# Short GpSimd steps behind each scatter of a routed result and behind some scatters in attention

## The reference

```
x = x + layernorm(attention(layernorm(x)))        # 16 heads, 4 key/value groups, rotary, causal softmax
h = layernorm(x)
gate = sigmoid(h @ gate_w + gate_b)               # 16 experts
values, chosen = top_k(gate, 2)                   # two experts per token, values scaled to sum 1
routed = sum over the two of value * (silu(h @ eg) * (h @ eu)) @ ed
x = x + layernorm(h + shared_mlp(h) + routed)
```

## Time and profile before

| | |
|---|---|
| median of 3 runs | 2366.59 us (2365.68 to 2369.12) |
| span of the profiled execution | 2472.9 us |
| the profiled execution's own time outside its span | not given by the page |
| busy share PE, DVE, POOL, ACT | 93%, 78%, 69%, 57% |
| mean granted TensorE clock | 0.980 |
| indirect DMAs issued by POOL | 256 in attention, 286 in the experts |

### The profile page before, as it was taken

One profiled execution on the slowest core, in us unless ns is written; L12 is line 12 of the kernel. 1 busy time (PEld: TensorE's weight loads), 2 busy tenths in 40 slices (PEclk: granted clock), 3 DMA queues, 4 the chain that ended last, 5 costly groups with the idle time before them and its releaser, 6 DMA issues.

```text
span 2472.9 us, 57907 instructions
## 1 busy us (share of the span) xinstructions
PE 2296.5 (93%) x17882; PEld 1478.5 (60%) x17882; DVE 1931.5 (78%) x5142; ACT 1399.3 (57%) x3208; POOL 1697.4 (69%) x2893
## 2 busy tenths in 40 slices
PE   5999999999999999999999999998789899999997
PEld 2565555555555555555555555554668787777754
DVE  6788888888888888888898888975455454677778
ACT  1565666656666566665666665665344454444444
POOL 4556777677776777777777767753656676777776
PEclk7999999999999999999999999998999999999999
DMA  4544445554455544445443444332344466788877
GB/s 133 136 140 147 144 133 156 155 165 138 138 155 146 165 137 142 133 138 157 122 132 111 141 137 129 113 100 70 114 142 146 136 190 201 250 278 283 273 257 253
DMA packets 289486, 391.76 MB, mean 158 GB/s; under 512 B 28000, under 2 KB 237920, under 8 KB 289056
## 3 DMA queue, kind: packets, MB, share of 16 engines
q1 hardware_dynamic: 263168, 316.72, 43.3%
q0 software_dynamic: 26016, 71.34, 7.9%
HBM read 186.84 MB, written 182.75 MB: 149 GB/s over the span
## 4 chain that ended last, share of the span: by engine, by line
PE 51%; POOL 26%; issue 8%; DVE 8%; ACT 3%; DMA 1%; another core or an unknown queue 1%; SPq 1%; POOLq 0%; ACTq 0%; DVEq 0%
PE bank L1710 9%; PE ps_a L859 6%; PE bank L1724 5%; PE ps_out L873 5%; PE ps_d L843 5%; PE ps_d L896 4%; POOL q_parts L683 4%; PE ps_d L889 4%; POOL sorted_dram L770 3%; PE bank L1691 3%; DVE roped_q L1124 3%; POOL rest L685 2%; POOL q_parts L685 2%; POOL guess L739 2%; PE ps_a L861 2%
## 5 line engine op out<-in xcount | busy, mean ns | idle before, releaser
L986 ACT ACTIVATE probs<-ps_a 128x512 f32<-128x512 f32 (+1 forms) x1408 | 713.1, 558 | 434.4 <-PE ps_a L861 339.4
L1109 DVE TENSOR_REDUCE negmax<-ps_d 128x2 f32<-128x768 f32 (+3 forms) x768 | 773.0, 1031 | 138.8 <-PE ps_d L845 73.8
L859 PE MATMUL ps_a<-qs,ks 99*128 99x512 bf16 (+3 forms) x2048 | 515.9, 302 | 19.2 <-ACT probs L986 15.6
L843 PE MATMUL ps_d<-ks,qs 96*128 96x128 bf16 (+3 forms) x2048 | 488.0, 304 | 22.1 <-DMA qs<-q_stack_dram 10.8
L845 PE MATMUL ps_d<-mask_max,ident_bf 128*128 128x128 bf16 x2048 | 394.9, 222 | 0.0
L861 PE MATMUL ps_a<-mask_exp,ident_bf 128*128 128x128 bf16 x2048 | 388.1, 220 | 0.0
L1621 POOL DMA_INDIRECT y_dram<-ysb,to_row x286 | 286.3, 1001 | 98.4 <-issue 53.5
L873 PE MATMUL ps_out<-probs,va 128*32 128x512 f32 (+3 forms) x4096 | 331.9, 442 | 4.1 <-DVE by_token L1159 4.1
L859 PEld LDWEIGHTS ps_a<-qs,ks 99*128 99x128 bf16 x2048 | 199.4, 98 | 202.7 <-ACT probs L986 66.6
L843 PEld LDWEIGHTS ps_d<-ks,qs 96*128 96x128 bf16 x2048 | 202.7, 99 | 191.1 <-DVE negmax L1109 40.6
L770 POOL DMA_INDIRECT sorted_dram<-h,slot x256 | 268.6, 1049 | 66.3 <-issue 65.4
(11 more groups left out here) (209 smaller groups left out, 4253.1 us busy)
## 6 DMA issues: line engine op xcount, KB each, us to landing
qs<-q_stack_dram SPq DMA_DIRECT2D x128, 384.0 KB
rows<-sorted_dram SPq DMA_DIRECT2D x286, 129.0 KB
y_in<-y_dram SPq DMA_DIRECT2D x32, 1024.0 KB
q_stack_dram<-q_parts SPq DMA_DIRECT2D x64, 384.0 KB, 3.0
x_in<-in_x SPq DMA_DIRECT2D x32, 512.0 KB, 4.3
q_stack_dram<-q_parts SPq DMA_DIRECT2D x64, 256.0 KB, 3.2
h_dram<-h SPq DMA_DIRECT2D x32, 512.0 KB
h<-h SPq DMA_DIRECT2D x32, 512.0 KB
```

Source lines behind the costliest of these rows:

```text
L843: pe.matmul(ps_d[:, number % 2, at:at + width], qs[0:KR, b % 2, h, j * P:(j + 1) * P], ks[0:KR, b % 2, g, 0:width], start=True, stop=False)
L859: pe.matmul(ps_a[:, number % 3, at:at + width], ks[0:KM, b % 2, g, j * P:(j + 1) * P], qs[0:KM, b % 2, g * HG + h0 + k, j * P:T], start=Tr ...
L986: act.activation(probs[:, at:at + nh * width], ps_a[:, number % 3, 0:nh * width], ACT.Exp) \
L1109: dve.tensor_reduce(negmax[:, g // 2, j, at:at + nh], src, AX_X, ALU.max, negate=True) \
```

## The change

A class `Spacing` issues a number of 1x1 steps on GpSimd. Each waits for the one before it (its own semaphore `spaced`), none waits for another engine or for a DMA. Two such steps follow the scatter of block j = 1 of every batch, and in the last two batches the scatters of all four blocks. One step follows each of the 286 scatters of a routed result. Nothing else is moved, and no other engine's program changes.

```
+class Spacing:
+    def __init__(self, pool, cell, zeros, done):
+        self.pool, self.cell, self.zeros, self.done, self.n = pool, cell, zeros, done, 0
+
+    def __call__(self, steps):
+        for _ in range(steps):
+            if self.n:
+                self.pool.wait_ge(self.done, self.n)
+            self.pool.tensor_tensor(self.cell, self.zeros, self.zeros, ALU.add).then_inc(self.done, 1)
+            self.n += 1
...
-        pool_cell, dve_cell = sb("pool_cell", [1, 2]), sb("dve_cell", [1, 2])
+        pool_cell, dve_cell = sb("pool_cell", [1, 3]), sb("dve_cell", [1, 2])
...
-        doubled = sem("doubled")
+        doubled, spaced = sem("doubled"), sem("spaced")
...
-        prepare_experts, tile_turn, rest_of_experts = gpsimd_experts(pool)
+        space = Spacing(pool, pool_cell[:, 2:3], zero_col[0:1, 0:1], v["spaced"])
+        prepare_experts, tile_turn, rest_of_experts = gpsimd_experts(pool, space)
...
                     out=sorted_dram[b // SPLIT_AT][:, :], in_=h2[:, k, j, :], in_offset=None,
                     out_offset=bass.IndirectOffsetOnAxis(ap=slot[b % 2][:, j, k:k + 1], axis=0),
                 ).then_inc(scattered[b % 2], 16)
+            if j == 1 or b >= B - 2:
+                space(2)
...
                 out=y_dram[:, :], in_=ysb[:, k, :], in_offset=None,
                 out_offset=bass.IndirectOffsetOnAxis(ap=to_row[k][:, 0:1].bitcast(U32), axis=0),
             ).then_inc(y_stored[k], 16)
+            space(1)
```

More of the change, by code:

```diff
@@ L1606, in sync_experts, with gpsimd_experts @@
         return turn, rest
-    def gpsimd_experts(pool):
+    def gpsimd_experts(pool, space):
         pause = Pause(pool, v["pool_cell"][:, 1:2], zero_col[0:1, 0:1], paused)
```

## The result

The changed kernel runs in 2370.28 us (median of 17 runs, 2367.15 to 2372.61), the kernel before, on the same chip, in 2365.68 us (17 runs, 2363.46 to 2369.12). The ratio is 1.0020, 95% interval 1.0014 to 1.0027: slower by 4.6 us, just about the 0.2% that a measurement can tell. My forecast was faster by 35 us. The time lies outside the forecast's own range (2308 to 2362) and inside the wider one (2303 to 2372) only because that one took in the first rival; it moved the other way than I forecast. And the profile says nearly the opposite of the runs.

The account below looks back on a forecast made before the run. Late signals behind POOL's close indirect DMAs were taken to delay line 687, which ends each attention batch. Gain 59 less 0.4 made 58.6 us of span; 0.6 of it, 35 us, off 2366.6 gave 2332 us, range 2308 to 2362.

Parts of the forecast that it names:

- first rival: Whole kernel: nothing to gain in the runs, only +0.4 us of cost, so 2367 us; chance 0.33.
- From the profiled execution to the runs: Step from profile to timed runs: of a possible 0 to 58.6 us, took 0.6, 35 us, giving 2332 us.
- late signals: PE's completions reaching VectorE and ScalarE late behind POOL's close indirect DMAs; waits of 77 + 20 = 97 us.
- What bounds the kernel: Attention, 52.0 us per batch: line 687's start ends last, released by POOL's root behind late moments and the second rotary product.
- The gain: Gaps let PE's signals through: 29 x 1.7 = 49 us in attention, 10 us at its end, 59 at most.
- The rule against the gain: DMA never contends with a compute engine at SBUF's ports; by it the gain is nil, 2367.0 us.
- The price of a pair: Two steps between two scatters in attention cost POOL about 0.44 us, between 0.36 and 0.50.
- Covered; price 0: Batches 0 to 28: POOL's 2.64 us wait for moments behind the scatters hides the pair's 0.44 us.
- if that cover were gone, 13 us: Batches 0 to 28: without POOL's wait for moments, the pairs would cost 29 x 0.44 = 13 us.
- The price at the end: Last batches of attention: +0.4 us for batch 29; 1.3 us of pairs ahead of other work in 30 and 31, covered.
- covered by PE as long as POOL keeps up: Experts' 286 single steps: price 0, with 0.9 us of room left in a finals' round of about 15.2 us.
- The second rival: Tiles beside finals, 2110 to 2370 us: POOL becomes the bound from 0.33 us per step; 17 us slower, 2384; chance 0.13.

## Why the prediction was wrong

**The step that failed** is "From the profiled execution to the runs". It took 0.6 of a gain that, in the runs, was 0. The paragraph had the right sum in it, 77 + 20 = 97 us of late signals that "would fit into the 106", and the sentence for this outcome, "If the span falls by some 58 us and the runs don't move, the late signals were the profiler's", and then set a share by choice. What the experiments showed: three profiles of before's instructions without one late signal, at spans of 2366.2 to 2366.6 us, so the whole 106 us belonged to the execution that I had read, and the share to take was 0. My first rival, 2367.0, has the effect right, and only a price missing.

**What bounds the kernel** was wrong with it. "What ends last in a batch is the start of line 687" is true of that execution only. In the undisturbed traces PE is busy 298.9 of 300 us in attention, and over the whole span 84% of the chain that ended last is PE's.

**The gain.** Its cause fell too. "Indirect DMAs close behind one another hold up signals" was read off a correlation in one execution. The kernels with no pairs have the same runs of scatters at the same distance, 1.27 us, and no late signal. The 107 us look like a confirmation, twice what I had forecast, and aren't one.

**The rule against the gain.** By the Trainium skill ("SBUF — State Buffer", Who interferes with whom) DMA never contends with a compute engine, and with that I had put the time at 2367.0. The undisturbed traces agree with the rule: PE at 298.9 of 300 us beside DMA at a share of 0.52.

**The price of a pair**, 0.44 us (0.36 to 0.50), measured 0.31: the distance of two scatters went from 1.27 to 1.58 us, as 0.14 of the next DMA's gap lies under the steps. "Covered; price 0" holds, with less to cover it than I thought: 0.31 us for moments and some of the 0.47 before line 687, not 2.64. Line 687's wait fell to 0.41, the period didn't change. That "if that cover were gone, 13 us" was the right doubt for six steps: 30 us.

**The price at the end** is the term that was put too low, and with no gain against it, it made the sign. I priced it +0.4 for batch 29 and wrote of the single steps "covered by PE as long as POOL keeps up". POOL keeps up as a whole, but in front of the last second root it has 14 stores, and the chain runs through them: 2.3 us, half of the 4.6. I had looked for waits behind the scatters, not for what stands ahead of a root in POOL's queue. The cover that I named behind batch 30's scatters, a wait of 8.2 us for moments, was the disturbed execution's too: it is 2.5 us in the other traces of before and 0.6 after. And the stores, "wanted eight tiles later", do hold VectorE up: it waits for one five times, 3.1 us in all, where before it never did. Of the other half 0.7 us has a place, in the first two batches; the rest, some 1.6 us, is within the error of the runs and stays open.

**The second rival** named the finals and 0.33 us per step. One step stays under it (0.14 where stores come close), and no wait of PE for the finals' results grew by more than 0.6 us (VectorE's sum, 1.4 to 2.0). The place that decides first is another: with two steps, 2.03 us a store against PE's 1.625 in the plain tiles, which I had used only as a sign that a distance of 1.63 does no harm.

## What to carry to other kernels

Compare a profile's span with the median of the runs before reading a single wait in it: one that is 4.5% longer has something that the runs don't, and as the waits that I had called late signals summed to about the difference (97 of 106 us), the right share to forecast from them was none. A second profile of the same program showed it here. Far more groups without a landing time than usual, here 13 against 2 to 6, go with it in this one case. A short instruction is free only where its engine's queue has a wait behind it before the next result that somebody needs; go through the queue from each such result backwards, above all where two phases overlap, and if a backlog of work that nobody waits for stands ahead of it, move the result's instructions ahead of the backlog.

## What was not expected of the hardware

The cost of 1x1 GpSimd steps between two indirect DMAs is far from even, and no run here shows why: 0.14 us for one behind a store that has a pause step ahead of the next (distance 1.355 to 1.50 us), 0.53 for a second (2.03), 0.26 for a third (2.29). With one step the gap before the DMA is as short as 0.16 us, with two it is 0.42 each time. And two profiled executions of one program can differ by 106 us, in late signals spread over all of attention and the first part of the experts, while the 17 other profiles, of it and of its relatives, show none.
